# Mixer's front: transposed input, statistics of all blocks early, input products inside a scan pair

## The reference, cut to what matters

```python
x = x + _layernorm(_L0_attn_ref(_layernorm(x, axis=-1), ...), axis=-1)
# _layernorm: (x - mean) / sqrt(var + 1e-5), over the 128 features

xz = x @ W_in.T                       # 128 -> 512
xc, z = split(xz, 2)
xc = silu(causal depthwise conv of 4 taps(xc) + conv_b)
dBC = xc @ W_x.T                      # -> delta (64), B (16), C (16)
delta = softplus(delta @ W_dt.T + b_dt)
deltaA = exp(delta[..., None] * A)    # A = -exp(A_log), 16 states
BX = delta[..., None] * Bm[:, :, None, :] * xc[..., None]
hs = associative_scan(h = deltaA * h + BX, over positions)
y = einsum('bldn,bln->bld', hs, Cm) + Dp * xc
out = y * silu(z) @ W_out.T
```

## Time and profile before

| | |
|---|---|
| Median of 3 runs | 1194.97 us (1193.07 to 1195.08) |
| Profiled execution, first to last instruction | 1192.5 us |
| PE, DVE, ACT, POOL busy | 1067.6, 1044.9, 1025.7, 872.6 us |
| DMA | 148.33 MB, mean 124 GB/s |

### The profile page before, as it was taken

How to read it: one execution, slowest core, us unless ns; L and a number is a source line. 1 busy time by engine, 2 the same in 40 slices (tenths; PEclk the granted TensorE clock), 3 DMA queues, 4 the chain that set the end, 5 groups by cost and what they waited for, 6 DMA issues and landing times. The chain is left out here.

```text
span 1192.5 us, 28322 instructions
## 1 busy us (share of the span) xinstructions
PE 1067.6 (90%) x8400; PEld 883.2 (74%) x8400; DVE 1044.9 (88%) x2028; ACT 1025.7 (86%) x2217; POOL 872.6 (73%) x682
## 2 busy tenths in 40 slices
PE   7799999999999999999999999977988876999990
PEld 3588787887878878788787887867555555999990
DVE  4799999999999999999999999999579888577773
ACT  4999999999999999999999998987389985678883
POOL 2589888897888988888788898987426665444455
PEclk9899999999999999999999999999899999999995
DMA  3433333333333333333333333344276656777640
GB/s 119 138 99 95 105 98 110 97 104 99 94 107 97 102 103 96 99 105 101 99 102 99 90 106 98 102 139 127 57 174 156 165 154 175 256 247 243 230 163 26
DMA packets 150484, 148.33 MB, mean 124 GB/s; under 512 B 46721, under 2 KB 100675, under 8 KB 150367
## 3 DMA queue, kind: packets, MB, share of 16 engines
q1 hardware_dynamic: 145022, 134.36, 37.9%
q0 software_dynamic: 5344, 12.63, 3.0%
HBM read 103.51 MB, written 23.17 MB: 106 GB/s over the span
## 5 line engine op out<-in xcount | busy, mean ns | idle before, releaser
L1108 POOL TENSOR_TENSOR cm<-rows_or_blocks 128x1024 f32<-128x1024 f32 x256 | 604.9, 2371 | 128.1 <-DVE rows_or_blocks L931 127.9
L931 DVE TENSOR_TENSOR_SCAN rows_or_blocks<-abuf,hstate,bank_pair 128x512 f32<-128x512 f32 x512 | 614.0, 1260 | 25.5 <-ACT abuf L740 9.6
L487 PE MATMUL bank_pair<-ident,cm 128*128 128x128 f32 x2048 | 255.0, 273 | 2.0 <-POOL cm L1108 2.0
L487 PEld LDWEIGHTS bank_pair<-ident,cm 128*128 128x128 f32 x2048 | 229.8, 141 | 3.6 <-POOL cm L1108 2.5
L467 PE MATMUL bank_pair<-ident,ub 128*128 128x128 f32 x1024 | 145.4, 279 | 35.1 <-ACT ub L751 17.6
L740 ACT ACTIVATE abuf<-delta,aneg 128x512 f32<-128x512 f32 x256 | 166.2, 709 | 1.9 <-DVE rows_or_blocks L931 1.8
L740 ACT ACTIVATE abuf<-xg_or_delta,aneg 128x512 f32<-128x512 f32 x256 | 166.2, 708 | 1.3 <-DVE xg_or_delta L911 1.3
L467 PEld LDWEIGHTS bank_pair<-ident,ub 128*128 128x128 f32 x1024 | 114.3, 141 | 70.9 <-DVE rows_or_blocks L931 31.5
L382 PE MATMUL bank_pair<-xnT,rows_or_blocks 128*128 128x512 f32 x256 | 124.4, 603 | 1.0 <-ACT halo L673 1.0
L2373 POOL DMA_INDIRECT out<-res,tokens x71 | 74.2, 1046 | 65.3 <-DVE res L2344 48.0
L751 ACT ACTIVATE ub<-vs_or_uT,bT 128x256 f32<-128x256 f32 x256 | 108.4, 495 | 0.2
(11 more groups left out here) (296 smaller groups left out, 1974.4 us busy)
## 6 DMA issues: line engine op xcount, KB each, us to landing
rows_or_blocks<-c_rows SPq DMA_DIRECT2D x256, 256.0 KB, 3.2
w_of_tile<-w SPq DMA_DIRECT2D x71, 256.0 KB, 2.9
rows_or_blocks<-routed SPq DMA_DIRECT2D x71, 128.5 KB, 2.2
xin<-in_x SPq DMA_DIRECT2D x16, 256.0 KB, 3.6
xres<-in_x SPq DMA_DIRECT2D x16, 256.0 KB, 3.8
x_rows<-x1t SPq DMA_DIRECT2D x16, 256.0 KB, 3.5
xg_or_delta<-x_rows SPq DMA_DIRECT2D x16, 256.0 KB
v_rows<-vs_or_uT SPq DMA_DIRECT2D x16, 256.0 KB
```

The lines of the kernel that those rows point to most:

```text
L487: mm = pe.matmul(ps_y[j // 2][:, (j % 2 * CH + c) * P:(j % 2 * CH + c + 1) * P], cm[:, n % CM_RING, c, j * P:(j + 1) * P], ident[:, :], is ...
L931: dve.tensor_tensor_scan(hbuf[:, n % RING, c, :], abuf[:, n % RING, c, :], ps_bx[n % 2 * CH + c][:, :], hstate[:, bass.ds(g * (NST * CH) + ...
L1108: pool.tensor_tensor(cm[:, n % CM_RING, :, :], hbuf[:, n % RING, :, :], c, ALU.mult).then_inc(s_cm, 1)
```

## The change

The caller passes x a second time, transposed (`xt`: 128 features by 3 + 512 positions for each block, the three before it included, zeros at a sequence's start). In the kernel:

- `xnT` is now xT times the reciprocal roots spread over all partitions. Blocks 0 and 1: TensorE spreads the roots into PSUM (`spread_rstd`), VectorE multiplies (`first_xnT`). Blocks 2 to 15: the roots lie as rows in DRAM (`rs`), SP loads xT and the spread row into `xf` (`load_xT`, one step ahead, n = 8), GpSimd multiplies (`normed`, n = 4).
- Statistics: rows of all 16 blocks are loaded at the start into the space of `cm` (`xrows`). Statistics of blocks 0 and 1 as before, of 2 to 7 in one go before `f_delta(0)`, of 8 to 15 one each at n = 1 to 8 of step 0. Roots of 2 to 7 in one `f_root` behind `decay(0, 0)`, of 8 to 15 at n = 11 of step 0; TensorE turns each set (`turn_rstd`), ScalarE copies (`copy_rsT`), SP stores (`store_rstd`).
- `turn_x`, `f_norm`, `f_xnT`, `halo`, `load_x` are gone.
- `input_product(g, n)` moves from behind both scans of state n - 1 to between them; that of state 0 to between the scans of state 15 of the step before.
- `split_biases` on VectorE now stands behind `first_xnT(1)`. Several semaphores are merged.

```diff
-        xin = sb("xin", [P, TT, D])
+        xf = sb("xT_and_rstd", [P, 2, TAPS - 1 + HALF])
+        xrows = cm[:, :, :, :].rearrange("p r c l -> p (r c l)").rearrange("p (f t d) -> p f t d", t=TT, d=D)
...
+        def stats_done(f):
+
+            return 2 * (f + 1) if f < 2 else 6 + 2 * max(f - LATE_STATS + 1, 0)
...
+            def load_xT(f):
+                sp_.wait_ge(s_xnT, f)
+                sp_.sem_inc(carrier, 1)
+                sp_.wait_ge(s_rs, 16 * (10 if past(f, 4) else 6))
+                sp_.sem_inc(carrier, 1)
+                sp_.dma_start(xf[:, 0, :], xt_t[bass.ds(f, 1)].rearrange("o p l -> (o p) l")).then_inc(s_xt[0], 16)
+                sp_.dma_start(xf[:, 1, :], rs[bass.ds(f, 1), :].rearrange("o l -> (o l)").partition_broadcast(P))\
+                   .then_inc(s_xt[0], 16)
+
+            def store_rstd(part):
+                sp_.wait_ge(s_rst, part + 1)
+                sp_.sem_inc(carrier, 1)
+                for t in range(TT):
+                    sp_.dma_start(rs[part * SEQS:(part + 1) * SEQS, BORDER + t * P:BORDER + (t + 1) * P],
+                                  rsT[part][t * BLK + part * SEQS:t * BLK + (part + 1) * SEQS, :]).then_inc(s_rs, 16)
...
-                    if n == (1 if past(g, 1) else 5) and has(g + 3):
-                        load_x(g + 3)
+                    if n == 8 and has(g + 3):
+                        load_xT(g + 3)
+                    if n == 14 and not past(g, 1):
+                        store_rstd(1)
...
-            load_x(1)
+            load_rows(1, 1, 2)
+            load_first_xT(1)
             load(w_out[:, :, :], w_out_t.rearrange("(c p) d -> p c d", p=P), s_wo)
             load(biases[:, :], biases_in, s_wo)
-            load_x(2)
+            load_rows(2, 2, LATE_STATS)
+            load_rows(3, LATE_STATS, STEPS)
...
             store_c(0)
+            store_rstd(0)
+            load_xT(2)
             run_steps(step, sp_)
...
+            def turn_rstd(part):
+                pe.wait_ge(s_frstd, 2 * part + 6)
+                if part == 0:
+                    pe.wait_ge(s_xnT, 2)
+                else:
+                    pe.wait_ge(s_ut, 2)
+                pe.transpose((ps_bx[2], m0)[part][:, 0:P], rstd[:, :, :].rearrange("p t f -> p (t f)"), ident[:, :])\
+                  .then_inc(s_avg, 1)
...
-                    if n == 3 and has(g + 2):
-                        turn_x(g + 2)
+                    if n == 12 and not past(g, 1):
+                        turn_rstd(1)
...
             f_xc(0, 0, range(TAPS))
+            spread_rstd(1)
             f_xc(0, 1, range(TAPS))
             pe.wait_ge(s_w, 16 * 3)
             f_dbc(0)
-            turn_x(1)
             turn_b(0)
             f_dt(0, 0)
             f_dt(0, 1)
             state_in(0, 0)
+            turn_rstd(0)
             f_xc(1, 0, range(TAPS))
             f_xc(1, 1, (0, 1))
             turn_u(0)
...
+            def copy_rsT(part):
+                act.wait_ge(s_avg, part + 4)
+                act.activation(rsT[part], (ps_bx[2], m0)[part][:, 0:P], ACT.Copy).then_inc(s_rst, 1)
...
-            f_xnT(1)
             f_bT(0)
...
             decay(0, 0)
+            f_root(2, 2, LATE_STATS)
+            copy_rsT(0)
             f_uT(0)
             scaled(0, 1)
...
+            def first_xnT(f):
+                dve.wait_ge(s_xt[f], 16)
+                dve.wait_ge(s_avg, f + 2)
+                dve.tensor_tensor(xnT[:, f, BORDER:], xf[:, f, BORDER:], ps_bx[2 + f][:, :], ALU.mult).then_inc(s_xnT, 1)
...
-                for c in (range(CH), reversed(range(CH)))[(n + 2) % NST in PRODUCT]:
+                for i, c in enumerate((range(CH), reversed(range(CH)))[(n + 2) % NST in PRODUCT]):
+                    if i == 1 and (n + 1) % NST in PRODUCT:
+                        if n < NST - 1:
+                            input_product(g, n + 1)
+                        elif has(g + 1):
+                            input_product(g + 1, 0)
...
-                    if isinstance(g, int) and (g, n) == (0, 1):
-                        f_stats(2)
-                    if n in PRODUCT:
-                        input_product(g, n)
+                    if not past(g, 1) and 1 <= n <= STEPS - LATE_STATS:
+                        f_stats(3, LATE_STATS + n - 1, LATE_STATS + n)
...
-                    if n == 10 and has(g + 3):
-                        f_stats(g + 3)
...
+            first_xnT(1)
             split_biases()
+            f_stats(2, 2, LATE_STATS)
             f_delta(0)
             first_u()
+            input_product(0, 0)
...
+            def normed(f):
+                pool.wait_ge(s_xt[0], 32 * f - 16)
+                pool.wait_ge(s_xc_mm, 2 * f - 2)
+                pool.wait_ge(s_z_mm, 2 * f - 2)
+                pool.tensor_tensor(xnT[:, parity(f), :], xf[:, 0, :], xf[:, 1, :], ALU.mult).then_inc(s_xnT, 1)
...
                 if past(k, CM_RING):
                     pool.wait_ge(s_y, k - CM_RING + 1)
+                else:
+                    pool.wait_ge(s_fstat, stats_done(2 * n + 1))
...
+                    if n == 4 and has(g + 2):
+                        normed(g + 2)
```

More of the change, by code:

```diff
@@ L125, in mamba @@
         yg = sb("yg", [P, CH, HALF])
+        rsT = [yg[:, c, 0:P] for c in range(CH)]
+        xrows = cm[:, :, :, :].rearrange("p r c l -> p (r c l)").rearrange("p (f t d) -> p f t d", t=TT, d=D)
         tsq = sb("tsq", [P, TT])
@@ L413, in turn_b @@
                 pe.wait_ge(s_split, f + 1)
-                if past(f, 1) and has(f + 1):
-                    pe.wait_ge(s_xnT, f + 2)
-                elif past(f, 1):
+                if past(f, 1):
                     pe.wait_ge(s_z, 2 * f)
@@ L636, in root, with f_root @@
             def root(out, var, s_out, count):
-                act.activation(out[:, :], var, ACT.Ln, bias=eps[:, 0:1]).then_inc(s_out, 1)
+                act.activation(out, var, ACT.Ln, bias=eps[:, 0:1]).then_inc(s_out, 1)
                 act.wait_ge(s_out, 2 * count + 1)
-                act.activation(out[:, :], out[:, :], ACT.Exp, scale=-0.5).then_inc(s_out, 1)
-            def f_root(f):
-                act.wait_ge(s_fstat, 2 * f + 2)
-                if not past(f, 1):
+                act.activation(out, out, ACT.Exp, scale=-0.5).then_inc(s_out, 1)
+            def f_root(i, first, last):
+                act.wait_ge(s_fstat, stats_done(last - 1))
+                if i == 0:
                     act.wait_ge(s_consts, 1)
-                root(rstd, mv[:, :, 1], s_frstd, f)
+                root(rstd[:, :, first:last], mv[:, first:last, :, 1].rearrange("p f t -> p t f"), s_frstd, i)
             def t_root(t):
@@ L822, in step @@
                         ahead(n)
-                    if n == 5 and has(g + 2):
-                        f_xnT(g + 2)
                     if n < NST - 1:
@@ L828, in step @@
                         decay(g + 1, 0)
-                    if isinstance(g, int) and (g, n) == (0, 2):
-                        f_root(2)
-                        f_norm(2)
+                    if n == 11 and not past(g, 1):
+                        f_root(3, LATE_STATS, STEPS)
+                    if n == 13 and not past(g, 1):
+                        copy_rsT(1)
                     if n == 1:
@@ L854, in step @@
                         t_root(g - 1)
-                    if n == 13 and has(g + 3):
-                        f_root(g + 3)
-                        f_norm(g + 3)
             act.preload_act_table_set(LN_SET)
-            f_root(0)
-            f_norm(0)
-            f_xnT(0)
+            f_root(0, 0, 1)
             act.wait_ge(s_wchan, 16)
-            act.activation(aneg[:, :, :], alog, ACT.Exp).then_inc(s_aexp, 1)
-            f_root(1)
-            f_norm(1)
+            act.activation(aneg[:, :, :], alog, ACT.Exp).then_inc(s_aneg, 1)
+            f_root(1, 1, 2)
             f_xc(0)
@@ L1184, in _ @@
             masks()
-            pool.wait_ge(s_sel0, 5)
+            pool.wait_ge(s_sel0, 6)
             run_steps(step, pool)
```

157 lines of the change are left out of this document (78 added, 79 removed).

## The result

The kernel after takes 1242.56 us (median of 4 runs, 1239.37 to 1248.23) where the kernel before takes 1195.03: a ratio of 1.0401, interval 1.0376 to 1.0426. The forecast was slower, at 1210 with a range up to 1215. The direction was right; two thirds of the loss were not in the sum.

What follows compares the result with a forecast made beforehand. GpSimd's loop through TensorE was taken to bound each mixer step, pitch 49.9 to 50.0 us. Start +15.2, 13 steps +1.5 and end -1.8 gave +15: span 1192.5 to 1207.5, plus 2.5, hence 1210; range 1184 to 1215.

Steps and rivals of the forecast that it cites:

- TensorE's run of 24.13, back to back: Each mixer step, from `turn_u` to the next step's first matmul of state 2: 24.13 us without a gap.
- product 4's hold: Each mixer step: product 4 between state 3's scans makes C product 4 on GpSimd start 1.5 us later.
- the loop over GpSimd: Each mixer step, through GpSimd's C products, `f_u` and TensorE: 13.3 + 12.57 + 24.13 = 50.0 us, +1.5 over 13 steps.
- The rival of a free GpSimd: Mixer steps: GpSimd's path doesn't bind, ScalarE's loop sets a pitch of 48.4 us; time 1189 us; chance 0.25.
- The rival of the loop's edge: VectorE's hardware-loop stall lands on scan 15: +1 us at each of five edges; 1216 us; dearer start's chance 0.07.
- The start: Up to step 1's first matmul of state 2: late root turn, slow clock and late statistics, +15.2 us.
- The five statistics groups between busy scans: Step 0 on VectorE: five of eight late statistics, 1.4 us each, don't fall into waits: 7.0 us.
- The tail: After step 14's first matmul of state 2, VectorE alone sets the time: eight products give 0.22 each, -1.8 us.

Runs made afterwards that it cites:

- a1: Kernel after with all input products back behind both scans, multiplication still at state 4: 1206.14 us, ratio 1.0095 to the kernel before.
- c1: Kernel after with only products 12 and 14 between scans, those of 0, 4 and 8 behind both: 1216.63 us, ratio 1.0170 to before.
- d1: Kernel after with only the product of state 0 between scans, the others behind both: 1207.28 us, ratio 1.0091 to before.
- a2: Kernel after with GpSimd's multiplication (`normed`) at state 2 instead of 4, all five products between scans: 1237.43 us, ratio 1.0358 to before.
- b1: Kernel before with only the input products moved between the two scans, nothing else of the change: 1223.89 us, ratio 1.0228 to before.
- a3: Kernel after with products behind both scans and GpSimd's multiplication at state 2 instead of 4: 1203.21 us, ratio 1.0057 to before.
- a5: Kernel after with products behind both scans, multiplication at state 2 and first roots turned late: 1195.62 us, ratio 0.9992 to before.
- f2: Against f1, one of the two late statistics groups at state 4 moved back (1, 1, 3, 1, 1, 1 at states 1 to 6): 1191.61 us, ratio 0.9964.
- f1: Against a5, step 0's eight late statistics groups put in VectorE's gaps (1, 1, 3, 2, 1 at states 1 to 5): 1191.73 us, ratio 0.9957.
- d2: Kernel after with only the product of state 4 between scans, the others behind both: 1226.38 us, ratio 1.0254 to before.
- c2: Kernel after with products 0, 4 and 8 between scans, those of 12 and 14 behind both: 1234.14 us, ratio 1.0314 to before.
- a4: Kernel after with `turn_rstd(0)` behind block 1's taps and `turn_u(0)`, its copy behind `scaled(0, 1)`: 1234.45 us, ratio 1.0339 to before.

## Why the forecast was off

**The step that failed: "TensorE's run of 24.13, back to back".** That row was read in step 13 of the kernel before, where no product stood between scans. I used product 4's hold for GpSimd and never asked what the other four holds do. Product 14 stretches the scans of state 13 and product 0 those of 15; TensorE's second halves of states 15 and 1 lie inside that very run. It measured 25.85 in the step shown, 1.72 more. All of that is at these two places: from the first half to the second it takes 1.32 and 1.29, where four such matmuls without a wait take 0.44 (505.84 to 506.28 in the same step). In the mean, turn_u to z is 23.53 where 24.13 less the 1.73 from z to S is 22.40: 1.13 a step, 15 over 13 steps, of an error of 21. The runs give the parts: 22.48 with no product between (a1), 0.70 by 12 and 14 (c1) and 0.35 by 0 (d1) make the 23.53.

**The step that held: the loop over GpSimd.** S to turn_u was forecast at 25.87 and measured 26.2 in the step shown, with TensorE waiting for GpSimd's u; in the mean z to turn_u is 28.12 against 27.60, 0.52 a step or 7 over 13 steps, the rest of the error. 0.22 of the 0.52 are the two falls of TensorE's clock, which the forecast didn't have. Of the 1.36 by which z to turn_u exceeds a1's, a2 shows 0.79 as the hold itself, the multiplication is 0.35 and the clock 0.22; b1 has 1.14 against the kernel before without any multiplication. That the multiplication costs nothing by itself and something once product 4 takes its gap away, as the forecast had it, is what a3 against a1 (0.00 a step) and a2 against after show; but its text lays the 1.5 to that lost gap, and the larger part is the hold.

**The balance of hold and gain.** My sum had the loop at 48.5 without the hold and at 50.0 with it: a gain of 1.4 a step and a cost of 1.5. a1 shows what the rest of the change gives: 49.24, a gain of 0.69. The hold costs 2.42. The 48.5 lay 1.4 under the 49.9 measured of the kernel before, and the forecast took the whole of that as gained; half of it came.

**The rival of a free GpSimd** gave a pitch of 48.4. a1 has exactly that in the steps outside the hardware loop (z to z 48.4 in steps 1, 2 and 13) and 49.0 to 49.8 inside it, but for 48.6 in its last step; every second step there ends with the stall at the loop's edge. The forecast's sign for it, that step 13 to 14 already runs at 48.3, holds from one `f_dt` to the next and not from z to z, which is 49.2 there in the kernel before. The rival's pitch was real, behind an order that this change doesn't have.

**The rival of the loop's edge** was right in kind: with product 0 between the scans of 15, +1.05 in the last part of the four steps that end at an edge (d1). Alone, most of it is given back. In the kernel after it isn't: it is the 0.35 a step above, some 4 us, where the rival had 5.

**The start** was forecast at +15.2 and came at +18.5. `uT(0)` was foreseen at 38.1 and stands at 39.78, the wait of TensorE and the taps at half speed as described; delta(1) at 76.2 against 77.6. One term was short by 1.3: delta(0) at 27.7 and not 26.4, with softplus and the six blocks' statistics both ending there. In the twelve kernels that are alike up to there it came anywhere from 25.9 (c1) to 27.7, so 1.3 lies within the spread of this start. From there to the first z the held scans of step 0 are 2.2 by a1, which the forecast had only for state 4. The five statistics groups between busy scans were put at 7.0; taking three of them into gaps, from a5 to f2, moved the first z from 94.6 to 89.0, 1.1 of it by an earlier delta(0): 1.5 for each group, near the 1.4 of the sum.

**The tail** was forecast at -1.8 from eight products at 0.22 less. With the products behind it is 99.0, as before, and 102.6 with them between. The 0.21 of idle time between a product and its own scan is there in a1 too, and ending it was worth nothing that shows.

**Behind the mixer** 4.9 more were measured and none foreseen. b1 has 4.6, a3 5.0, a1 3.3, a5 2.2, f1 1.5 and f2 1.0, though nothing behind the mixer differs among the kernels of the change and b1 has there the program of the kernel before. Each is one profiled execution, and those of the kernel before alone had spans from 1190.9 to 1199.5. So it isn't shown that the change makes this term; it stays open.

## What to carry to other kernels

A half that is released scan by scan is a pipeline with another engine: what stands between the two scans is on that engine's path, even if both orders have the same work. Before filling a bubble of 0.2 us, list who waits for the second instruction, and price the filler at its whole length there. And where a sum uses a run "back to back", check that each of its inputs is still made in the kernel after as it was where the run was read. Two edits that share a gap are to be costed together: here the multiplication was free only without product 4's hold.

## What the runs showed of the hardware

I had not expected TensorE's clock to fall in the middle of a steady mixer. Windows of d2 (length, busy time of each engine, then the granted clock) across the two waits at state 5:

```profile
569.10:571.40 2.30, 1.13 (x8) 0.90 (x9) 2.30 (x3) 2.30 (x5) 0.37 (x1) 1.00 0.43 114
571.40:575.20 3.80, 3.80 (x16) 3.05 (x15) 3.80 (x4) 3.80 (x8) 3.80 (x4) 0.55 0.10 36
575.20:579.00 3.80, 3.80 (x29) 3.21 (x28) 2.00 (x3) 3.46 (x8) 3.80 (x3) 1.00 0.25 82
```

```profile
571.41 1.71 PE L532 MATMUL bank_pair<-ident,ygT 128*128 128x128 f32 x8
...
573.77 1.65 PE L463 MATMUL bank_pair<-dbc,w_dt 65*128 65x512 f32 x2
```

TensorE idled 0.80 and 1.16 within 3 us, was granted 1.2 GHz for most of the next 3.8 (0.55 in the mean of that window), and the same eight transposes took 1.71 instead of 1.04. From 100 to 779 us, d2 has seven such episodes, c2 four, the kernel after two and a4 two, b1 one; before, a1, c1 and d1 have none. The Trainium skill (TensorE: Matmul & The Clock Gate, Part 1) says that idling throttles TensorE, and the trace agrees in that every fall in these steps follows the two waits; but the kernel after has the same 0.80 and 1.16 in step 5, with a fall, and in step 8, shown above, without one. So in this case the pair of waits doesn't decide it, and what does is open. The price differs: in the kernel after and in c2 a fall costs up to 1.3 us of its step (pitch 52.5 against 51.2 in steps 5 and 11); in d2 the steps from 457 to 661 with it have a pitch of 51.0, those from 255 to 457 without it 50.6.

Where it comes in a chain that nothing covers, it is dear: f1 against f2 above, some 2.4 us at the first z from a statistics group or two moved by a state.
